# A graph layer's first stage: 113-row transfers split into 112 and 1 rows, and level 0's work moved ahead among the one-hots

## The reference

```python
h = _layernorm(x); xs = [h]
for W, b in ((W0, b0), (W1, b1), (W2, b2)):
    m = concatenate([h[dst], h[src] - h[dst]], axis=-1) @ W + b
    h = relu(segment_sum(m, dst, 625) / maximum(count(dst), 1)[:, None]); xs.append(h)
x = x + concatenate(xs, axis=-1) @ Wf + bf
g = _layernorm(x)
top2 = one_hot(top_k(g @ Wg + bg, 2)).sum()
x = x + sum over experts e of top2[:, e] * (gelu(g @ W1[e] + b1[e]) @ W2[e] + b2[e])
```

## Time and profile before

| | us |
|---|---|
| median of 3 runs (lowest, highest) | 177.0 (176.54, 177.05) |
| the profiled execution's own time | 177.12 |
| its span, first to last instruction | 175.3 |
| busy in the span: PE, PEld | 143.2, 120.1 |
| busy in the span: DVE, ACT, POOL | 89.3, 65.3, 74.8 |

### The profile page before, as it was taken

The page is one execution under the profiler, slowest core; times in us unless marked ns, Lnnn a source line. Parts: engine busy times, 40 slices in busy tenths (PEclk is TensorE's granted clock), DMA queues, the critical chain, the costliest instruction groups (busy, mean ns, idle before and its releaser), DMA issues.

```text
span 175.3 us, 3032 instructions
## 1 busy us (share of the span) xinstructions
PE 143.2 (82%) x971; PEld 120.1 (69%) x972; DVE 89.3 (51%) x235; ACT 65.3 (37%) x183; POOL 74.8 (43%) x99
## 2 busy tenths in 40 slices
PE   1353384999999999989999948989999999999710
PEld 1332272998899899979999936857666666766600
DVE  6689999778799650305036885622222222223100
ACT  8333876467312140315030480323443333334200
POOL 6804930000499049950000200075555666663662
PEclk9999999999999999999999999999999999999995
DMA  4629999990000789400000432014244333332332
GB/s 146 194 28 310 369 366 366 368 316 12 6 0 4 204 299 327 142 4 0 0 0 4 134 128 97 0 60 90 30 71 79 64 62 60 60 64 30 60 60 30
DMA packets 16055, 20.33 MB, mean 116 GB/s; under 512 B 1754, under 2 KB 12388, under 8 KB 15908
## 3 DMA queue, kind: packets, MB, share of 16 engines
q1 hardware_dynamic: 13492, 16.54, 29.0%
q0 software_dynamic: 2544, 3.54, 12.0%
HBM read 16.81 MB, written 3.26 MB: 115 GB/s over the span
## 4 chain that ended last, share of the span: by engine, by line
PE 63%; DMA 11%; DVE 11%; issue 5%; POOL 3%; ACT 2%; POOLq 1%; SPq 1%; ACTq 0%; DVEq 0%
PE cnt_ps L1658 9%; PE bank L1639 6%; PE bank L1509 6%; DMA x_sb<-in_x 5%; PE cnt_ps L1509 4%; PE g_ps L1639 4%; PE g_ps L1344 3%; PE g_ps L1345 3%; PE g_ps L1346 3%; PE cnt_ps L1652 3%; DMA out_rows<-y_sb,row_put 2%; DMA out_rows<-y_sb,row_of 2%; DVE hot_lo L971 2%; PE cnt_ps L1344 2%; DMA xg<-x_rows,row_of 2%
## 5 line engine op out<-in xcount | busy, mean ns | idle before, releaser
L1658 PE MATMUL cnt_ps<-w_sb,h_t 128*128 x104 | 24.7, 380 | 1.1 <-ACT h_t L886 1.1
L1658 PEld LDWEIGHTS cnt_ps<-w_sb,h_t 128*128 128x128 f32 x104 | 18.8, 190 | 3.8 <-issue 1.8
L652 POOL DMA_INDIRECT out_rows<-y_sb,row_of x10 | 15.9, 1591 | 12.5 <-DMA out_rows<-y_sb,row_of 9.9
L646 POOL DMA_INDIRECT xg<-x_rows,row_of x12 | 12.1, 1005 | 18.6 <-DVE row_of L1313 15.2
L1400 PE MATMUL bank<-hot_key,hot_lo 125*128 125x45 bf16 (+4 forms) x80 | 8.3, 243 | 11.6 <-DVE hot_key L974 7.5
L1400 PEld LDWEIGHTS bank<-hot_key,hot_lo 125*128 125x128 bf16 x80 | 5.3, 123 | 13.9 <-DVE hot_key L974 13.0
L971 DVE TENSOR_TENSOR hot_lo<-iota_lo,edge_rel 125x1024 bf16<-125x1024 int16 x20 | 13.9, 697 | 1.6 <-PE g_ps L1400 1.5
L1282 DVE TENSOR_TENSOR y_sb<-cnt_ps,b_bc 128x256 f32<-128x256 f32 x13 | 5.5, 424 | 17.6 <-PE cnt_ps L1658 17.6
L1639 PE MATMUL bank<-w_sb,xt 128*128 x28 | 13.4, 600 | 0.7 <-ACT xt L890 0.5
L1278 DVE TENSOR_TENSOR h_pre<-bank,b_bc 128x512 f32<-128x512 f32 x7 | 4.8, 692 | 13.8 <-PE bank L1639 13.8
L882 ACT ACTIVATE h_act<-h_pre 128x512 f32<-128x512 f32 x13 | 8.2, 630 | 9.3 <-DVE h_pre L1278 9.3
(11 more groups left out here) (299 smaller groups left out, 405.0 us busy)
## 6 DMA issues: line engine op xcount, KB each, us to landing
w_sb<-in_L_ffn_W SPq DMA_DIRECT2D x16, 512.0 KB, 10.2
b_bc<-in_L_ffn_b SPq DMA_DIRECT2D x8, 256.0 KB, 4.8
w_stage<-in_L_gnn_W SPq DMA_DIRECT2D x3, 512.0 KB, 6.2
w_stage<-in_L_gnn_Wf SPq DMA_DIRECT2D x4, 256.0 KB, 7.5
b_bc<-in_L_ffn_b SPq DMA_DIRECT2D x1, 1024.0 KB, 8.4
x_rows<-x_f SPq DMA_DIRECT2D x1, 640.0 KB, 3.3
x_sb<-in_x SPq DMA_DIRECT2D x1, 512.0 KB
out_rows<-x_sb SPq DMA_DIRECT2D x1, 512.0 KB
```

What stands on the lines that cost most here:

```text
L646: pool.indirect_dma_start(out=xg[:, b, :], out_offset=None, in_=x2_rows, in_offset=bass.IndirectOffsetOnAxis(ap=rows, axis=0)).then_inc(x_ ...
L652: pool.indirect_dma_start(out=out, out_offset=bass.IndirectOffsetOnAxis(ap=rows, axis=0), in_=y_sb[:, b, :], in_offset=None, compute_op=AL ...
L1658: last = pe.matmul(bank[3][:, 0:D], h_t[:, k, :], w2_sb[:, ds(e, 1), k, :], start=k == 0, stop=k == HC - 1)
```

## The change

Each transfer of 113 rows (x in, and the sum out) becomes one of 112 rows (`EVEN`) and one of a single row. The statistics of x move on VectorE from behind `hot_pair(3)` to behind `hot_pair(1)`; the largest `dst` per row, which stood there, follows them. The root, the normalized rows, the upper and lower halves and the transposes move ahead likewise on ScalarE, VectorE and TensorE, one between two pairs. The third part of the weights (Wf's) is split after the first two and counted by itself, so that `w_split` runs one higher and SP's reload waits for one count more. The nine products start behind pair 20 instead of pair 26 and stand between single pairs. `add_halves(0)` moves behind `hot_pair(18)`. Nothing is computed otherwise. The diff, cut to its core:

```diff
+EVEN = LAST // 16 * 16
...
-            sp.dma_start(x_sb[0:LAST, NT - 1, :], x[(NT - 1) * P:NODES, :]).then_inc(x_in, 16)
+            sp.dma_start(x_sb[0:EVEN, NT - 1, :], x[(NT - 1) * P:(NT - 1) * P + EVEN, :]).then_inc(x_in, 16)
+            sp.dma_start(x_sb[EVEN:LAST, NT - 1, :], x[(NT - 1) * P + EVEN:NODES, :]).then_inc(x_in, 16)
...
-                sp.wait_ge(w_split, l)
+                sp.wait_ge(w_split, l + 1)
...
-            sp.dma_start(out[(NT - 1) * P:NODES, :], x1_sb[0:LAST, NT - 1, :]).then_inc(x1_stored, 16)
+            sp.dma_start(out[(NT - 1) * P:(NT - 1) * P + EVEN, :], x1_sb[0:EVEN, NT - 1, :]).then_inc(x1_stored, 16)
+            sp.dma_start(out[(NT - 1) * P + EVEN:NODES, :], x1_sb[EVEN:LAST, NT - 1, :]).then_inc(x1_stored, 16)
...
-            pool.wait_ge(x1_stored, 48)
+            pool.wait_ge(x1_stored, 64)
...
-            write_chunks(0, 0, 8)
-            key_table(2)
-            act.wait_ge(edge_col_done, 3)
-            act.copy(edge_key[:].rearrange("p (q j) -> p q j", j=EH), edge_cols(1)).then_inc(edge_key_done, 1)
-            act.wait_ge(var_ready, 1)
-            act.activation(std[:], var_eps[:], ACT.Sqrt).then_inc(std_ready, 1)
...
-            write_chunks(1, 8, 16)
-            act.wait_ge(rstd_ready, 1)
-            xn_row(0)
+            starts = chunk_starts(0)
+            write_pair(0, 0, starts[0:2])
+            write_pair(0, 2, starts[2:4])
+            act.wait_ge(var_ready, 1)
+            act.activation(std[:], var_eps[:], ACT.Sqrt).then_inc(std_ready, 1)
+            write_pair(0, 4, starts[4:6])
+            key_table(2)
+            write_pair(0, 6, starts[6:8])
+            act.wait_ge(edge_col_done, 3)
+            act.copy(edge_key[:].rearrange("p (q j) -> p q j", j=EH), edge_cols(1)).then_inc(edge_key_done, 1)
+            act.wait_ge(w_in[0], 32)
+            w_upper(0)
+            starts = chunk_starts(8)
+            for j in range(4):
+                write_pair(1, 8 + 2 * j, starts[2 * j:2 * j + 2])
+                if j == 0:
+                    act.wait_ge(rstd_ready, 1)
+                xn_row(j)
+            xn_row(4)
             starts = chunk_starts(16)
-            for j in range(4):
-                write_pair(1, 16 + 2 * j, starts[2 * j:2 * j + 2])
-                xn_row(1 + j)
+            write_pair(1, 16, starts[0:2])
             key_table(3)
+            write_pair(1, 18, starts[2:4])
             act.wait_ge(w_diffed, 1)
+            w_upper(1)
+            write_pair(1, 20, starts[4:6])
+            write_pair(1, 22, starts[6:8])
             starts = chunk_starts(24)
-            for j in range(4):
-                write_pair(2, 24 + 2 * j, starts[2 * j:2 * j + 2])
-                if j < 3:
-                    w_upper(j)
+            write_pair(2, 24, starts[0:2])
+            ht_upper(0)
+            write_pair(2, 26, starts[2:4])
+            ht_upper(1)
+            w_upper(2)
+            write_pair(2, 28, starts[4:6])
+            ht_upper(2)
+            write_pair(2, 30, starts[6:8])
+            ht_upper(3)
             key_table(4)
-            starts = chunk_starts(32)
-            for j in range(4):
-                write_pair(2, 32 + 2 * j, starts[2 * j:2 * j + 2])
-                ht_upper(j)
...
+            rest = write_units(2, 20)
+            ys_upper(0, 0)
+            write_rest(2, 22, rest)
+            ys_upper(0, 1)
+            act.wait_ge(b0_in, 16)
             rest = write_units(3, 24)
+            own0_out(0)
             write_rest(3, 26, rest)
-            ys_upper(0, 0)
+            ys_upper(0, 2)
             rest = write_units(3, 28)
-            act.wait_ge(b0_in, 16)
-            ys_upper(0, 1)
-            own0_out(0)
+            own0_out(1)
             write_rest(3, 30, rest)
-            ys_upper(0, 2)
+            ys_upper(0, 3)
             rest = write_units(4, 32)
-            own0_out(1)
-            ys_upper(0, 3)
+            own0_out(2)
             write_rest(4, 34, rest)
-            own0_out(2)
+            ys_upper(0, 4)
             rest = write_units(4, 36)
-            ys_upper(0, 4)
+            own0_out(3)
             write_rest(4, 38, rest)
-            own0_out(3)
...
-            chain(dve.tensor_reduce(span[:, 1:2], dst_nat[:], AX.XY, ALU.max))
-            dve.tensor_scalar(span_diag[:, 1, :], ident[0:EQ, 0:EQ], span[:, 1:2], None, ALU.mult)\
-                .then_inc(span_ready, 1)
-            hot_pair(2)
-            hot_pair(3)
-
-            dve.wait_ge(x_in, 32)
+            dve.wait_ge(x_in, 48)
...
+            chain(dve.tensor_reduce(span[:, 1:2], dst_nat[:], AX.XY, ALU.max))
+            dve.tensor_scalar(span_diag[:, 1, :], ident[0:EQ, 0:EQ], span[:, 1:2], None, ALU.mult)\
+                .then_inc(span_ready, 1)
+            hot_pair(2)
+            dve.wait_ge(std_ready, 1)
+            dve.reciprocal(rstd[:], std[:]).then_inc(rstd_rough, 1)
+            hot_pair(3)
+            dve.wait_ge(span_ps, 2)
+            read_span(1, ALU.max, max_read)
             dve.wait_ge(tables, 3)
             dve.wait_ge(edge_col_done, 3)
             hot_pair(4)
-            dve.wait_ge(std_ready, 1)
-            dve.reciprocal(rstd[:], std[:]).then_inc(rstd_rough, 1)
-            dve.wait_ge(span_ps, 2)
-            read_span(1, ALU.max, max_read)
-            hot_pair(5)
-            hot_pair(6)
             dve.wait_ge(w_in[0], 32)
             dve.tensor_tensor(w_stage[:, 0, :, :], w_stage[:, 0, :, :], w_stage[:, 1, :, :], ALU.subtract)\
                 .then_inc(w_diffed, 1)
-            hot_pair(7)
-            dve.wait_ge(tables, 4)
-            hot_pair(8)
-            hot_pair(9)
-            hot_pair(10)
-            for i in range(3):
+            hot_pair(5)
+            hot_pair(6)
+
+            def w_lower(i):
                 dve.wait_ge(w_hi_done, i + 1)
-                last = dve.tensor_tensor(w_lo[:, 0, :, i * D:(i + 1) * D], w_stage[:, (1, 0, 2)[i], :, :],
+                return dve.tensor_tensor(w_lo[:, 0, :, i * D:(i + 1) * D], w_stage[:, (1, 0, 2)[i], :, :],
                                          w_hi[:, 0, :, i * D:(i + 1) * D].bitcast(f32), ALU.subtract)
-            last.then_inc(w_split, 1)
-            hot_pair(11)
-            dve.wait_ge(tables, 5)
-            hot_pair(12)
-            for i in range(4):
+
+            def ht_lower(i):
                 (a, b), c = HALVES[Z_OUT[i][0]], Z_OUT[i][1]
                 dve.wait_ge(ht_hi_done, i + 1)
                 dve.tensor_tensor(ht_lo[:, c, a:b], xn_bank(i), ht_hi[:, c, a:b].bitcast(f32),
                                   ALU.subtract).then_inc(ht_ready, 1)
 
+            hot_pair(7)
+            dve.wait_ge(tables, 4)
+            w_lower(0)
+            hot_pair(8)
+            hot_pair(9)
+            w_lower(1).then_inc(w_split, 1)
+            ht_lower(0)
+            ht_lower(1)
+            hot_pair(10)
+            ht_lower(2)
+            ht_lower(3)
+            hot_pair(11)
+            dve.wait_ge(tables, 5)
+            hot_pair(12)
+            w_lower(2).then_inc(w_split, 1)
...
+            ys_lower(0, 0)
             hot_pair(13)
+            ys_lower(0, 1)
             hot_pair(14)
             hot_pair(15)
-            ys_lower(0, 0)
+            ys_lower(0, 2)
             dve.wait_ge(tables, 6)
             hot_pair(16)
-            ys_lower(0, 1)
             hot_pair(17)
-            ys_lower(0, 2)
+            ys_lower(0, 3)
+            hot_pair(18)
             add_halves(0, SPLIT_CHUNK)
-            hot_pair(18)
-            ys_lower(0, 3)
             hot_pair(19)
...
-            for u in range(16, 20):
-                sum_unit(u)
...
+            def xn_transposes(i):
+                h, c = Z_OUT[i]
                 a, b = HALVES[h]
                 for t in range(a // P, b // P):
                     pe.wait_ge(xn_ready, t + 1)
                     last = pe.transpose(xn_bank(i)[:, t * P - a:(t + 1) * P - a], xn[:, t, c * P:(c + 1) * P], ident[:])
                 last.then_inc(xn_t_done, 1)
+
             def sum_pair(u):
                 sum_unit(u)
                 sum_unit(u + 1)
 
-            for u in range(20, 28, 2):
-                sum_pair(u)
+            sum_pair(16)
+            xn_transposes(0)
+            xn_transposes(1)
+            sum_pair(18)
+            xn_transposes(2)
+            xn_transposes(3)
+            sum_pair(20)
             pe.wait_ge(w_split, 1)
             pe.wait_ge(ht_ready, 4)
             ys_product(0, 0)
+            sum_pair(22)
+            ys_product(0, 1)
+            sum_pair(24)
+            own0_product(0)
+            sum_pair(26)
+            ys_product(0, 2)
             sum_pair(28)
-            ys_product(0, 1)
-            own0_product(0)
-            sum_pair(30)
-            ys_product(0, 2)
-            sum_pair(32)
             pe.wait_ge(ys_ready, 1)
             own0_product(1)
+            sum_pair(30)
             pe.wait_ge(ys_ready, 2)
             ys_product(0, 3)
```

(15 more changed lines are left out.)

## The result

The changed kernel is slower: 178.29 us median (177.11 to 182.78, 17 runs) against 177.54 (176.54 to 181.02, 17 runs) for the kernel before on the same chip. The ratio is 1.0062 with a 95% interval of 1.0035 to 1.0088, some 1.1 us; the forecast was 175.1 and the range ended at 177.0. The profiled execution took 178.14, of it 176.3 span, against 177.12 and 175.3.

The account below looks back on a forecast made before the run. Bound: the chain of waits from the late 113-row x transfer to the first add_halves(1) at 44.52. VectorE's idle, 1.15 + 2.20 - 0.67 - 0.65 = 2.03 us, comes off 177.12, giving 175.1; range 173.8 to 177.0.

Parts of the forecast that it names:

- The split: Load of x: 112 rows plus one land by 7.5 at the latest, so VectorE's statistics at 8.57 don't wait.
- rival B: Load of x: the split brings x no earlier, 11.9; 3.3 lost against 2.03 won, 178.4 us; chance 0.12 with other late x.
- The extra issue: On SP, the split's added transfer issue costs 0.41 us and moves all later loads by that.
- GpSimd's chain ... takes 3.48, so xn may start at 15.87: Reciprocal to first normalized row: the chain keeps its 3.48 us after moving, so the row starts at 15.87.
- Idle up to pair 13, 0.67: VectorE up to one-hot pair 13: idle falls from 1.15 to 0.67 us, so pair 13 may start at 28.97.
- From pair 13 to 19: VectorE's waits there fall from 2.20 to 0.65 us; TensorE's products start about 25.7 and its pace rises near 30.
- rival C: TensorE's products of level 0: the slow pace lasts until about 34, VectorE sees some 1.1 us, 176.2 us; chance 0.15.
- Rival D: Degree sums: TensorE's pace falls after its rest from 39.6 to 42.7, costing 2.1, 177.2 us; chance 0.06 with no change.
- Behind 45 us nothing takes it back: After 45 us: GpSimd's split of level 1's weights and TensorE's level 0 products move together, so the gain stays whole.
- the sum of 2.03: Total forecast gain in us up to add_halves(1): 1.15 + 2.20 - 0.67 - 0.65.

Follow-up runs that it names:

- e4: The kernel before with only the transfers split into 112 and 1 rows, no order changed; ratio 0.9984 to the kernel before.
- e6: The changed kernel with VectorE waiting for GpSimd's shift ahead of pair 4; four executions took 178.6 to 183.6 us, no ratio.
- e2: The changed kernel with Newton's step and the shift on VectorE instead of GpSimd; ratio 0.9991 to the kernel before.
- e1: The changed kernel with 28 unused bf16 products on TensorE, 14 ahead of pair 38 and 14 behind it; ratio 1.0145 to the kernel before.
- e5: The changed kernel with the 113-row transfers unsplit again, the order alone; ratio 1.0229 to the kernel before.
- e14: The changed kernel with GpSimd's table, read only by the general path, moved behind its split of level 1's weights; ratio 1.0090 to the kernel before.
- e11: e4 with GpSimd's general-path table moved behind its split of level 1's weights; ratio 0.9887 to the kernel before.
- e3: The changed kernel with both the edits of e1 and e2, filler products and Newton on VectorE; ratio 1.0113 to the kernel before.
- e15: The same program as e11, measured once more on another run's chip; ratio 0.9945 to the kernel before.
- e7: e2 with TensorE's last three products one pair later, own0_product(3) behind the last pair as before the change; ratio 0.9984 to the kernel before.
- e10: e7 with GpSimd's general-path table moved behind its split of level 1's weights; ratio 0.9906 to the kernel before.
- e8: e4 with Newton's step and the shift on VectorE, in the order of before; ratio 1.0002 to the kernel before.

## Why the prediction was wrong

1. **The split: right.** x was there by 8.34, rival B did not come. The Trainium skill ("DMA: Bandwidth & Descriptors", Why a DMA increments its semaphore by 16 and not by 1) expects 112 rows to spread where 113 do not; e4, where the statistics lose their wait, agrees. The same page's advice against splitting in two (Rules for kernel authors) rests on both halves spraying; the 113 rows did not (DMA share 0.07), and it did not hold for this transfer. The extra issue did not move all later loads by 0.41: Wf was issued at 3.46, where it was 4.32.
2. **"GpSimd's chain ... takes 3.48, so xn may start at 15.87": the step that failed first.** I took a duration from one place and moved the chain beside other VectorE instructions. It took 5.74, 3.36 of it one product; e6 shows that VectorE caused this, e2 that the chain is worth 0.7%. The prediction named slowed one-hots beside GpSimd, but not the other direction. The Trainium skill ("SBUF — State Buffer", Who interferes with whom) says that a VectorE instruction with two inputs in SBUF contends with a GpSimd instruction that reads it, under an exclusive lock. The trace agrees as to the two engines. It does not show why GpSimd got no turn between two VectorE instructions: in the kernel before VectorE had no gap either, and the six operations took 0.20 to 0.69 each, as in all six profiles with GpSimd's chain in the old order. One difference stands in the rows: wherever the product took 3.36 or 3.37 (after, e1, e5, e14) it started 0.01 us after a `hot_lo`, and before it started in the middle of a `hot_key`. No run tests whether that decides.
3. **Idle up to pair 13, 0.67: mis-sized** as a consequence (its own terms add up to 0.45 to 0.65). It was 2.45 at pair 7 and 0.51 at `ht_lower`, and pair 13 started at 30.82, not 28.97.
4. **From pair 13 to 19: the pace.** The waits of `ys_lower` went. Those of one-hots came to 1.30 (0.79 and 0.51), where I had 0.65 in all. The products started at 27.77, not 25.7, and TensorE's pace rose near 32.4, not near 30: a part of rival C. In e1_fill, where TensorE was fast from the first product, these waits were 0.28 and `add_halves(1)` came 1.27 earlier. I had taken the moment of the rise from one profile; in the profiles here it lies anywhere from before 28 (e1) to about 36.2 (e11), and the same instructions have it at different times. How it is spread over the executions that were only timed is not known.
5. **Rival D, told at 2.1 us and given almost no chance, came.** The rest before the degree sums was named rightly; the clock was at the lower level from 46 to 49.5, and level 1 followed `add_halves(1)` 0.92 us later than before. The argument against it was one stretch in which TensorE had rested as long and the clock held. In ten of the seventeen profiles (e1, e3 to e6 and e11 to e15) the clock fell in that same stretch of the program, and e7 and e10 with nearly equal rests at 41 to 44 went apart. So a rest of this size may cost the clock in one execution and not in another; one row of its holding was no price of zero.
6. **"Behind 45 us nothing takes it back": wrong.** The clock took it: in e2 and e7 `add_halves(1)` came 1.27 and 1.34 us earlier than before, level 1 only 0.33 and 0.42, with the clock at the lower level between 44 and 48. GpSimd's split does start with the same `a_added`, as I wrote. But wherever TensorE came early it waited for that split, 0.40 to 0.76 us (the split's end at 56.0 to 57.5). In the kernel before the two came nearly together (57.05, the split's end at 56.93), and the first product followed the split's end by 0.56, as in e4 and e8: the split was the bound at level 1 there already.

In the profiled execution the 1.0 us of span arose so: +0.13 up to `add_halves(1)`, +0.92 from there to level 1's first product (13.89 against 12.97), -0.27 from there to `x1`, the rest behind. That e10's span lies 2.1 us under that of before (173.2 against 175.3), near the sum of 2.03, is luck: its `add_halves(1)` came 1.46 earlier and not 2.03, the rest was won up to level 1, where the prediction saw nothing to win, and over its executions the ratio gives 1.7. How much of the 1.1 us each cause holds alone isn't settled: e2 repairs the first and not the second, no run repairs the second without moving TensorE's code or its products, and TensorE's pace up to 36 us differs from one execution to the next.

## What to carry to other kernels

A duration taken from a trace holds for the company in which it was measured: before moving a chain of short GpSimd operations, look at what VectorE runs beside the new place, price the chain with a range, or let VectorE do the operations. A stage emptied of work ahead of a dense one is a cost as well, when TensorE rests in it. Before a milestone of one profile is compared with that of another, compare the duration of one and the same matmul in both: the pace alone moved one here by 1.3 us. And a gain at one milestone is not yet a gain at the end: follow it to the next ones, and ask which engine comes second.

## What the runs showed of the hardware that was not expected

- One GpSimd product of 128x5 took 3.36 us beside VectorE's instructions without a gap (after, e1, e5; 3.37 in e14), and 0.20 with VectorE at rest (e6), but 0.20 also in the kernel before, beside other VectorE instructions without a gap. In e6 VectorE then lost in its turn: a one-hot of 125x1024 took 1.10 in place of 0.68 beside GpSimd's bias split.
- The same instructions up to `add_halves(1)` ended at 44.65 (after), 44.50 (e14) and 43.38 (e1): a matmul of 256 columns took 415 to 416 ns from 28 to 32 us in the first two and 281 in the third.
- TensorE's stall at level 2 (0.62) moved and grew to 1.50 with eight instructions added 65 us earlier.
- With the one-engine transfer gone, the two weight loads behind it landed sooner: W0 in 4.8 and Wf in 5.3 us from issue, where W0 took 6.2 and Wf 9.2 before:

```profile
w_stage<-in_L_gnn_W SPq DMA_DIRECT2D x1, 512.0 KB, 4.8
w_stage<-in_L_gnn_Wf SPq DMA_DIRECT2D x1, 256.0 KB, 5.3
```
